# Two deformable layers on one core: packed storage of the bounded offsets, another way in for the first batch, and a later fourth band

## The reference

```
off = conv2d(x, ow, ob)                    # 9 taps x (dy, dx) per pixel
cy, cx = pixel + tap + off                 # where each tap samples
samp = bilinear sample of x at (cy, cx)    # 4 neighbours, zero outside the image
out = einsum('bckhw,ock->bohw', samp, w)   # 9 taps x 16 channels -> 16 channels
```

## Time and profile before

| | us |
|---|---|
| median of 3 runs | 729.74 (726.46 to 733.1) |
| the profiled execution | 729.7 |
| its span in the trace | 727.5 |
| VectorE busy | 600.2 (82%) |
| TensorE busy | 576.0 (79%) |
| ScalarE busy | 453.1 (62%) |
| GpSimd busy | 146.1 (20%) |

### The profile page before, as it was taken

The page is one execution under the profiler, slowest core; times in us unless marked ns, Lnnn a source line. Parts: engine busy times, 40 slices in busy tenths (PEclk is TensorE's granted clock), DMA queues, the critical chain, the costliest instruction groups (busy, mean ns, idle before and its releaser), DMA issues.

```text
span 727.5 us, 29228 instructions
## 1 busy us (share of the span) xinstructions
PE 576.0 (79%) x13258; PEld 413.8 (57%) x13258; DVE 600.2 (82%) x853; ACT 453.1 (62%) x803; POOL 146.1 (20%) x258
## 2 busy tenths in 40 slices
PE   2719999999888698888886788669888888659491
PEld 1205887775654477666665454357666666537380
DVE  6998999942459999999998443999999999884866
ACT  2776774233227789999983412669999899251514
POOL 1005000010241343344200025134334420000000
PEclk9959999999988899999999798979999999969696
DMA  5004000000669898888730066979888862000003
GB/s 215 0 9 109 4 5 20 4 5 20 168 219 386 246 310 276 277 276 274 247 130 2 3 178 216 379 235 306 279 287 283 279 222 112 3 1 5 1 4 116
DMA packets 30198, 111.16 MB, mean 153 GB/s; under 512 B 11140, under 2 KB 15940, under 8 KB 25976
## 3 DMA queue, kind: packets, MB, share of 16 engines
q0 software_dynamic: 14912, 87.85, 35.8%
q1 hardware_dynamic: 15160, 21.42, 9.7%
HBM read 92.25 MB, written 19.65 MB: 154 GB/s over the span
## 4 chain that ended last, share of the span: by engine, by line
DVE 38%; PE 36%; DMA 10%; ACT 6%; issue 5%; SPq 2%; POOL 1%; DVEq 0%; ACTq 0%; POOLq 0%
PE psum L1433 12%; DVE arena L820 8%; DVE arena L822 7%; DVE arena L823 7%; DMA arena<-offsets_by_batch 7%; PE psum L1487 6%; PE psum L1642 6%; DVE arena L812 3%; PE psum L1521 3%; ACT arena L1212 2%; PE psum L1451 2%; PE psum L1652 2%; DMA offsets_by_batch<-offsets 1%; PE psum L1391 1%; SPq L520 1%
## 5 line engine op out<-in xcount | busy, mean ns | idle before, releaser
L1521 PE MATMUL psum<-arena 64*64 64x297 f32 (+4 forms) x4512 | 223.1, 340 | 48.3 <-DVE arena L823 40.9
L1521 PEld LDWEIGHTS psum<-arena 64*64 64x64 f32 x4512 | 171.1, 136 | 106.8 <-DVE arena L823 49.6
L1737 POOL DMA_DIRECT2D arena<-offsets_by_batch x128 | 78.1, 624 | 200.0 <-DVE arena L823 130.1
L1239 ACT ACTIVATE arena<-psum 128x396 f32<-128x396 f32 (+1 forms) x192 | 86.1, 509 | 36.4 <-PE psum L1521 24.0
L1487 PE MATMUL psum<-arena 32*32 32x512 f32 x2304 | 88.3, 651 | 22.7 <-issue 16.9
L820 DVE SCALAR_TENSOR_TENSOR arena<-arena 128x396 f32<-128x396 f32 (+1 forms) x192 | 98.2, 554 | 3.5 <-ACT arena L1226 2.5
L1433 PE MATMUL psum<-arena 32*32 32x512 f32 x2592 | 93.6, 597 | 0.0
L822 DVE SCALAR_TENSOR_TENSOR arena<-arena 128x792 f32<-128x792 f32 (+3 forms) x96 | 92.3, 961 | 0.0
L823 DVE SCALAR_TENSOR_TENSOR arena<-arena 128x792 f32<-128x792 f32 (+3 forms) x96 | 92.2, 960 | 0.0
L1545 PE MATMUL psum<-arena 64*64 64x256 f32 x1152 | 83.1, 381 | 2.6 <-ACT arena L1242 2.2
L1487 PEld LDWEIGHTS psum<-arena 32*32 32x32 f32 x2304 | 49.3, 107 | 59.3 <-issue 44.9
(11 more groups left out here) (169 smaller groups left out, 640.8 us busy)
## 6 DMA issues: line engine op xcount, KB each, us to landing
arena<-offsets_by_batch POOLq DMA_DIRECT2D x112, 576.0 KB, 7.9
arena<-offsets_by_batch POOLq DMA_DIRECT2D x16, 624.0 KB, 7.6
offsets<-arena SPq DMA_DIRECT2D x32, 256.0 KB, 10.0
offsets_by_batch<-offsets SPq DMA_DIRECT2D x184, 24.0 KB
arena<-columns POOLq DMA_DIRECT2D x24, 160.0 KB, 9.3
columns<-arena POOLq DMA_DIRECT2D x8, 320.0 KB, 6.7
arena<-in_x SPq DMA_DIRECT2D x4, 512.0 KB, 5.3
out<-arena SPq DMA_DIRECT2D x8, 256.0 KB, 2.2
```

The costliest lines, as they stand in the source:

```text
L1239: ins = a.activation(ap(to + half * 2 * K * SX, [[SR, 2], [SX, 2 * K], [1, w]]), ap_ps(bank, [[CH, 2], [w, 2 * K], [1, w]], half * 2 * K * ...
L1521: ins = t_.matmul(ps_t(s, bank + r, first * K * w, many * K * w), window, ap(g_at(unit, d0) + first * TW + s * w, [[GS + TW, many], [SLOTS ...
L1737: g.dma_start(cols(in_at(n, 0), 2 * in_rows(n) * W, 64 * r + 32 * half, 32), bass.AP(batch_d.tensor, 2 * (4 * r * NB + n) * INS, [[0, QW / ...
```

## The change

It alters both deformable layers in the same way.

- The DRAM tensor of offsets holds 9 taps per image instead of 16 slots, and each plane has a row above and one below the image, stored once as zeros (four DMAs near the start). A store of a band is now eight DMAs of nine partitions. Arranging needs six DMAs for every batch but the first (eight, each with one more piece) and the last (eight).
- For band 0, SyncE stores the x axis and ScalarE the y axis, between two of its column copies; SyncE and ScalarE each arrange one axis of batch 0 (four DMAs each), and SyncE loads it by four DMAs of 64 partitions. GpSimd has no part in batch 0.
- Other batches are loaded by GpSimd in eight DMAs, four for x and then four for y, with a semaphore for each axis.
- Bands 0 to 2 are bounded by one VectorE instruction behind an additional ScalarE pass (a ReLU with another bias, four instructions); band 3 keeps the two instructions.
- Band 2 is bounded and reached behind batch 0, band 3 behind batch 4. TensorE runs band 3 tap by tap, one tap behind each of units 0 to 8, then the whole contraction of the first pair behind units 10 and 11; ScalarE copies band 3 ahead of unit 9's samples.
- GpSimd stores the second part of the columns only behind the issue of batch 1's loads. SyncE's order of stores and arrangements changes.

```
         def store_part(eng, L, m, axis):
             for h in range(2):
                 for b in range(2):
                     eng.dma_start(... [[PLANE, K], [2 * K * PLANE, 4], [1, CH]] ..., K)
         def arrange_first(eng, axis):
             for ky, at, step, row, rows in ((-1, 0, SLOTS, 1, SLOTS), (0, 3 * SLOTS, SLOTS, 0, SLOTS),
                                             (1, 6 * SLOTS, SLOTS, -1, SLOTS), (-1, KR, 1, 0, 1)):
                 eng.dma_start(...).then_inc(s_af[axis], 16)
         def load_first(eng, axis):
             for r in range(2):
                 eng.dma_start(cols(in_at(0, axis), ER * W, 64 * r, 64), ...).then_inc(s_fl[axis], 16)
 # SyncE
             for L in range(2):
                 store_offsets(L, 0)
-                arrange_batch(L, 0)
+                sp.wait_ge(s_ds[0], 128 * (L + 1))
+                arrange_first(sp, 0)
+                sp.wait_ge(s_af[0], 64 * (L + 1))
+                load_first(sp, 0)
+                sp.wait_ge(s_af[1], 64 * (L + 1))
+                load_first(sp, 1)
                 arrange_batch(L, 1)
                 arrange_batch(L, 2)
                 store_offsets(L, 1)
+                arrange_batch(L, 3)
+                arrange_batch(L, 4)
                 store_offsets(L, 2)
-                arrange_batch(L, 3)
+                for n in range(5, 9):
+                    arrange_batch(L, n)
                 store_offsets(L, 3)
 # VectorE, bound_offsets
+                if m < 3:
+                    dve.wait_ge(s_cvb, 3 * L + m + 1)
+                    v.scalar_tensor_tensor(d1, d1, con("twice_limit"), ..., ALU.min, ALU.add).then_inc(s_d1, 1)
+                    return
 # VectorE, layer2
-                for m in (1, 2):
-                    bound_offsets(L, m)
-                    reach(L, m)
+                bound_offsets(L, 1)
+                reach(L, 1)
 ...
                     if n == 0:
+                        bound_offsets(L, 2)
+                        reach(L, 2)
+                    if n == 4:
+                        dve.wait_ge(s_cve, 16 * (L + 1))
+                        reach(L, 3)
                         bound_offsets(L, 3)
-                        reach(L, 3)
 # ScalarE, copy_offsets
+                if m < 3:
+                    for i in range(4):
+                        act.wait_ge(s_cv, 16 * L + 4 * m + i + 1)
+                        ins = a.activation(cols(bounded_at(m) + i * CH, CH), ps(conv_bank(m) + i, 0, CH), ACT.Relu,
+                                           bias=cols(OBL + L, 1))
+                    ins.then_inc(s_cvb, 1)
 # ScalarE, the layer
                 copy_offsets(L, 0)
                 for g_ in (0, 2, 4, 6):
+                    if g_ == 2:
+                        act.wait_ge(s_d1, 4 * L + 1)
+                        store_part(a, L, 0, 1)
                     copy_columns(L, g_)
+                act.wait_ge(s_ds[0], 128 * (L + 1))
+                arrange_first(a, 1)
                 copy_offsets(L, 1)
-                copy_offsets(L, 2)
                 distances(L, 0)
                 for unit in range(RING):
                     y_terms(L, unit)
                 spread_windows(L, 0)
-                copy_offsets(L, 3)
+                copy_offsets(L, 2)
 # TensorE
-                convolve(3)
-                pe.wait_ge(s_cve, 16 * (L + 1))
                 for unit in range(UNITS):
                     sample(unit)
+                    if unit < OWN_TAPS:
+                        pe.wait_ge(s_cve, 16 * L + 12)
+                        convolve(3, unit, unit + 1)
+                    if unit in (OWN_TAPS + 1, OWN_TAPS + 2):
+                        pe.wait_ge(s_cve, 16 * (L + 1))
+                        contract(0, 0 if unit == OWN_TAPS + 1 else 5, 5 if unit == OWN_TAPS + 1 else K)
-                    if n >= 2 and 2 * step < K:
+                    if n >= 4 and 2 * step < K:
 # GpSimd
-                for half in range(2):
-                    for r in range(2):
-                        g.dma_start(cols(in_at(n, 0), 2 * in_rows(n) * W, 64 * r + 32 * half, 32), ...)
+                for axis in range(2):
+                    load_part(g, n, axis)
 ...
                 store_columns(L, 0)
+                load_windows(L, 0)
+                load_batch(L, 1)
                 store_columns(L, 1)
-                load_windows(L, 0)
-                load_batch(L, 0)
                 load_windows(L, 1)
-                load_batch(L, 1)
```

More of the change, by code:

```diff
@@ L122, in constants @@
     put("ramp", np.where(p[:, None] < 64, ramp, 0.0))
+    put("bounded_ramp", np.where(p[:, None] < 64, ramp - XLIM, -YLIM))
+    put("twice_limit", np.where(p[:, None] < 64, 2 * XLIM, 2 * YLIM))
     put("minus_q", -(p[:, None] % 64 // 4))
@@ L166, in vec @@
             return cols(VE + o + i, n, 0, pn)
-        SMALL = place(720)
+        SMALL = place(704)
         small_at = [SMALL]
@@ L316, in conv_bank @@
         def conv_bank(m):
-            return 4 if m % 2 == 0 else 0
+            return 0 if m == 1 else 4
         HALF = N // 2
@@ L359, in build @@
         OBQ = small(4)
+        OBL = small(2)
         COUNT = small(1)
@@ L472, in row_parts, with bounded_at, store_part, arrange_first @@
                      ap_ps(bank, [[SX, rows], [1, WB[2]]], rho * SX + 2 * WB[0])))
+        def bounded_at(m):
+            return RAW + NATS if m == 3 else D1 + m % 2 * NATS
+        def store_part(eng, L, m, axis):
+            for h in range(2):
+                for b in range(2):
+                    eng.dma_start(bass.AP(off_d.tensor, (axis * B + b) * K * PLANE + W + (2 * m + h) * CH,
+                                          [[PLANE, K], [2 * K * PLANE, 4], [1, CH]]),
+                                  ap(bounded_at(m), [[CH, 4], [1, CH]], 64 * axis + Q * h + KP * b, K)
+                                  ).then_inc(s_ds[m], 16)
+        def arrange_first(eng, axis):
+            for ky, at, step, row, rows in ((-1, 0, SLOTS, 1, SLOTS), (0, 3 * SLOTS, SLOTS, 0, SLOTS),
+                                            (1, 6 * SLOTS, SLOTS, -1, SLOTS), (-1, KR, 1, 0, 1)):
+                eng.dma_start(bass.AP(batch_d.tensor, (axis * ER + at) * W, [[2 * NB * INS, B], [step * W, 3], [1, rows * W]]),
+                              bass.AP(off_d.tensor, (axis * B * K + 3 * (ky + 1)) * PLANE + (row + 1) * W,
+                                      [[K * PLANE, B], [PLANE, 3], [1, rows * W]])).then_inc(s_af[axis], 16)
+        def load_first(eng, axis):
+            for r in range(2):
+                eng.dma_start(cols(in_at(0, axis), ER * W, 64 * r, 64),
+                              bass.AP(batch_d.tensor, 2 * 4 * r * NB * INS + axis * ER * W,
+                                      [[0, QW], [2 * NB * INS, 4], [1, ER * W]])).then_inc(s_fl[axis], 16)
+        def load_part(eng, n, axis):
+            for half in range(2):
+                for r in range(2):
+                    eng.dma_start(cols(in_at(n, axis), in_rows(n) * W, 64 * r + 32 * half, 32),
+                                  bass.AP(batch_d.tensor, 2 * (4 * r * NB + n) * INS + axis * in_rows(n) * W,
+                                          [[0, QW // 2], [2 * NB * INS, 4], [1, in_rows(n) * W]])
+                                  ).then_inc(s_in[n % 3][axis], 16)
         UNITS = NB * NU
+        PLANE = (H + 2) * W
+        OWN_TAPS = NU * 3
         @block.sync
@@ L490, in _ @@
                                  cols(T_PAD[3], H * C, 0, 4 * HALO)).then_inc(s_zp, 16)
+            for axis in range(2):
+                for row in (0, H + 1):
+                    sp.dma_start(bass.AP(off_d.tensor, axis * B * K * PLANE + row * W, [[PLANE, B * K], [1, W]]),
+                                 cols(T_PAD[0], W, 0, B * K)).then_inc(s_oz, 16)
             for pair in (0, 2):
@@ L629, in _ @@
                                       ALU.mult)
+            for L in range(2):
+                ins = v.tensor_tensor(cols(OBL + L, 1), cols(OB + L, 1), con("limit"), ALU.add)
             ins.then_inc(s_ob, 1)
@@ L1223, in y_terms @@
                 n, u = divmod(unit, NU)
+                if u == 0:
+                    act.wait_ge(s_in[n % 3][1] if n else s_fl[1], in_count(L, n))
                 if unit >= RING:
@@ L1275, in _ @@
                     if unit == 2 * NU:
-                        for m in range(4):
-                            act.wait_ge(s_ds[m], 64 * (L + 1))
+                        for m in range(3):
+                            act.wait_ge(s_ds[m], 128 * (L + 1))
+                        act.wait_ge(s_red, 4 * L + 3)
+                    if unit == 9 * NU:
+                        act.wait_ge(s_ds[3], 128 * (L + 1))
                         act.wait_ge(s_red, 4 * (L + 1))
+                    if unit == OWN_TAPS:
+                        copy_offsets(L, 3)
                     copy_samples(L, unit)
@@ L1285, in _ @@
                         spread_windows(L, n + 2)
-                    if u == NU - 1 and n % 2 == 1 and n >= 3:
-                        copy_rows(L, n // 2 - 1)
```

(14 more changed lines are left out.)

70 lines of the change are left out of this document (34 added, 36 removed).

## The result

The changed kernel takes 736.08 us (median of 9 runs, 732.83 to 741.01), the one before 729.51 in the same comparison: a ratio of 1.0099, 95% interval 1.0062 to 1.0136. It is 1% slower; 717.2 was forecast, in a range of 705 to 733. The profiled spans are 734.0 and 727.5 us.

The account below looks back on a forecast made before the run. The prediction took VectorE to bound the loops and a chain of waits on transfers to set the way in. It summed 729.7 - 24.8 (starts) + 9.3 (VectorE's loop) + 3 (TensorE's loop) = 717.2 us, range 705 to 733.

Parts of the forecast that it names:

- What bounds the kernel: VectorE bounds both loops, with only 3.5 and 2.4 us idle per 141 us; in the way in nothing is saturated.
- Bounding, ScalarE's issues, stores: Way in: bounding 2.35 us instead of 3.7, ScalarE's four issues 2.9, stores landed 4 us behind the last issue.
- Rival A: Way in: nine-partition stores still land at 8 us, so arranging starts 4 us later; 720.4 us, chance 0.14.
- The load: Way in: batch 0's load in four DMAs of twice the partitions takes 10 us, batch 0 there at about 209.
- Starts: First product of batch 0 comes 11.4 us earlier in layer one and 13.4 in layer two: -24.8 us.
- VectorE's moved work, +9.3: VectorE's loop: band 2's bound and reach, formerly in idle time, lie behind batch 0, 4.6 us a layer.
- TensorE's loop, +3: Units 0 to 8 fit (30 us against VectorE's 33); lag at units 10 and 11 costs 1.5 us a layer.
- Rival B: TensorE, at a low clock, bounds the first nine units: 734 us, or 726 with half the units; chance 0.16.
- The column store: GpSimd's second part of the columns arrives about 226, hidden or just not; wrong if unit 0's samples wait beyond 230.
- ScalarE's cluster at the batch's end: ScalarE's work at the batch's end, placed beside the lag of up to 4.6 us at units 10 and 11.
- Rival C: Mid-loop: GpSimd's eight load issues, if 1.06 us apart or more, make y late; one us late gives 741; chance 0.12.
- Rival D: The way in doesn't move, transfers trading places in saturated DMA engines: 733.6 us at worst, about 728 halfway; chance 0.08.

Follow-up runs that it names:

- experiment 6: In the version with band 3 ahead of the loop and GpSimd's batch 0 load, band 2 handled ahead of batch 0: 723.84 us; behind: 722.96; both 0.990.
- all three suspects out: Changed kernel without eight of band 3's nine taps, all but one tap of the first contraction, and most of band 3's raw copy: 723.75 us, 0.989.

## Why the prediction was wrong, by its own steps

**What bounds the kernel: right.** VectorE's idle time in the loop was scarce, and what was put ahead of it counted in full.

**Bounding, ScalarE's issues, stores: right, a little better than forecast.** The one-pass bounding took 2.35 us, the four issues 2.75, the stores landed 3.0 us behind their last issue (191.21 less 188.24; forecast 4). Rival A falls as a result, though nine engines or sixteen can't be told from one landing: the eight column stores of the kernel before weren't beside it. Arranging took 8.0 us until x's load (191.21 to 199.20), not 4.8, since an issue took 1.3 to 1.4 us instead of 0.70. That the load of x still began 18.6 us behind band 0's copy, where 17.4 was forecast, is in part luck: the stores had landed 2.0 us earlier than forecast, and the arrangement took 3.2 longer.

**The load: wrong in size.** Bounds of 8.1 and 14.5 us were given and 10 taken, "nearest the median landing". x was there 11.6 us and y 16.6 us behind the first issue: y beyond the upper bound. The median was of another shape and queue. The change's shape runs at half the rate, which no row of before shows.

**Starts: 24.8 forecast, 18.7 measured.** Band 1 ended earlier than forecast in both layers. In layer one its copy began at 198.6 instead of 203.6; in layer two its first pass ended 20.7 us behind band 0's copy, where 23.9 was taken. The forecast had also counted a copy twice there: it took the end of band 1's copy for its last product and added both passes behind it. VectorE and ScalarE were ready; the load became what batch 0 waits for.

**VectorE's moved work, +9.3: right as a price**, and repaid at the start, as experiment 6 shows for the version with GpSimd's load.

**TensorE's loop, +3: the step that failed.** It said that TensorE's 30 us and VectorE's 33 fit, and put the lag at units 10 and 11. Measured, the y waits behind batch 0's first product are 7.6 us in layer one and 10.4 in layer two, against 2.5 in the two layers together before: 15.5 us more, where +3 was forecast. The contraction cost nothing; the taps cost 10 to 12 us, and ScalarE's copy 4. The mistake was to compare totals of engines. A product's y terms wait for TensorE's samples of the unit three before, and in ScalarE's own order for its copy of them; TensorE's samples wait for the unit's products and for ScalarE's copy of the samples two before. That is a loop over three engines of three units' length; a tap of 1.2 us between two samplings lengthens it each time, and the slack of 4.6 us of bounding lay behind batch 0 alone, before the loop had run. The runs show what the taps and the copy cost; that the ring is the way by which they cost it is read from the program's order, and no run changes the ring.

**Rival B** named TensorE's taps, by a low clock, for 9 us a layer. In layer one the clock was low only at the beginning: 0.50, the lower of its two levels (1.2 of 2.4 GHz), between 218 and 224 us of the trace, behind 8.7 us without work, and 1.00 from 230 to 282, where the waits are. So its place was right, and there the waits need no low clock. In layer two it may have a share. The granted clock fell again where the waits are:

```profile
493.00:497.00 4.00, 4.00 (x76) 2.11 (x72) 1.25 (x3) 1.75 (x3) 3.72 (x7) 0.67 1.03 400
...
505.00:509.00 4.00, 2.81 (x40) 2.09 (x44) 1.20 (x3) 4.00 (x8) 2.41 (x5) 0.61 0.81 322
```

Both stretches lie partly at the lower level. TensorE had stood idle for 2.96 and 2.63 us just before these two stretches. Over 489 to 523 us the clock was 0.90 with TensorE busy for 29.1 us, so by an estimate from these figures the low clock cost it about 3 us there; it can be an effect of the lateness as well as a cause. In the kernel before the clock was 0.74 between 230 and 250 us, with y waits of 2.3 us in the whole layer.

**The column store**, one of the forecast's signs of being wrong, was at its edge. ScalarE's first copy of samples began at 229.99 us in layer one, where about 226 was forecast, after 2.46 us of idle time (1.96 in layer two). TensorE had unit 0's samples ready at about 224, and the only other thing the program waits for there is the second part of the columns, whose last store had been issued by 223.12. VectorE's wait right behind it was 0.2 us. Whether this adds to the waits of batches 2 to 4 no run separates; the 2.7 and 1.4 us left with all three suspects out are open.

**ScalarE's copy ahead of unit 9** was not costed at all; the forecast named "ScalarE's cluster at the batch's end" and left the new member out of it. It cost 4 us.

**Rival C: refuted.** GpSimd's eight issues take more of its time (211 us busy instead of 146), but batches 5 to 15 take 98.2 and 98.7 us against 98.6 and 98.1. **Rival D** holds for the loads in part: the engines were full, though with a slow shape rather than with traffic.

## What to carry to other kernels

Where engines hand units round a ring, cost an insertion by the longest way round for one unit, with the queue of each engine in its order, not by the busy time of each engine: 1.2 us behind each of eight units on an engine that was waiting at times cost 10 to 12 us in two layers. Work that is moved off an idle stretch into a saturated loop gains only as much as it brings the loop forward, less its own length; here the two were equal. And a load in a new shape, from a new queue, is a new price: put the old one's rate at one end of the range and half of it at the other.

## What the runs showed of the hardware

- A load of 64 partitions from rows repeated sixteenfold moved 220 to 230 GB/s with the DMA engines busy throughout, from SyncE and from GpSimd; one of 32 partitions from rows repeated eightfold moved 408 GB/s from GpSimd (with the next batch's loads behind it; 425 in the kernel before), and from SyncE 213 at a share of 0.51.
- Arrangement DMAs from two queues at once took 1.3 and 1.4 us an issue (1.2 to 1.5 in five later runs), eight from SyncE alone 1.0, the following twelve 0.65.
- Pieces of TensorE's idle time for "issue" in a way in (one of 4.75 us in the run with band 3 ahead) were gone in layer one when the load left half of the DMA engines' time free. In layer two of that run three pieces of 0.3 to 1.2 us were left. That the two are cause and effect is not shown; it rests on this one profile.
